# A Mamba block with a mixture of experts on one core: one buffer of delta*u, a last input in four pieces, and the slots of the chunks dealt anew

## What is computed

```python
u, res = split(x @ W_in)                     # 512 channels each
u = silu(three-tap causal convolution of u)
dt, Bm, Cm = split(u @ W_x)                  # 16 + 16 + 16
delta = softplus(dt @ W_dt + b_dt)
for each of 16 states n, along the tokens:
    h_n = exp(delta * A_n) * h_n + (delta * u) * Bm_n
    y  += h_n * Cm_n
y = (y + u * D) * silu(res)
x = layernorm(x + y @ W_out)
```

## Time and profile before

| what | value |
| --- | --- |
| median of 3 runs | 2394.84 us (2394.42 to 2395.79) |
| the profiled execution | 2394.69 us, its span 2392.8 us |
| chunks 0 to 15, first scan to last | 25.2 to 1562 us |
| granted clock of TensorE | 0.977 of full speed, mean over the span |
| busy over the span | PE 94%, PEld 76%, DVE 90%, ACT 73%, POOL 77% |

### The profile page before, as it was taken

One profiled execution on the slowest core, in us unless ns is written; L12 is line 12 of the kernel. 1 busy time (PEld: TensorE's weight loads), 2 busy tenths in 40 slices (PEclk: granted clock), 3 DMA queues, 4 the chain that ended last, 5 costly groups with the idle time before them and its releaser, 6 DMA issues. The chain is left out here.

```text
span 2392.8 us, 39513 instructions
## 1 busy us (share of the span) xinstructions
PE 2245.3 (94%) x14183; PEld 1809.9 (76%) x14183; DVE 2145.2 (90%) x2917; ACT 1746.1 (73%) x2935; POOL 1851.2 (77%) x1028
## 2 busy tenths in 40 slices
PE   9999999999999999999999997745999999999995
PEld 5677777777777777777777766634999999999995
DVE  6999999999999999999999999986787787787775
ACT  6989989999899999998998998842344344434355
POOL 5899999999999999999999999952336437436465
PEclk9999999999999999999999999966999999999998
DMA  3222222222122222221222211122122322322353
GB/s 114 63 62 72 72 80 71 72 71 81 62 72 72 80 71 72 71 81 62 72 72 80 72 63 62 62 71 75 32 67 45 87 65 45 88 64 44 89 200 135
DMA packets 88722, 178.93 MB, mean 75 GB/s; under 512 B 9152, under 2 KB 51904, under 8 KB 88528
## 3 DMA queue, kind: packets, MB, share of 16 engines
q1 hardware_dynamic: 73648, 154.11, 19.4%
q0 software_dynamic: 14880, 22.29, 5.2%
HBM read 140.20 MB, written 36.18 MB: 74 GB/s over the span
## 5 line engine op out<-in xcount | busy, mean ns | idle before, releaser
L1105 DVE TENSOR_TENSOR_SCAN hst<-da,dbu 128x512 f32<-128x512 f32 x1008 | 1173.4, 1209 | 15.5 <-ACT da L806 10.1
L612 POOL TENSOR_TENSOR dbu<-du,b_all 128x2048 f32<-128x2048 f32 x254 | 1154.5, 4546 | 22.3 <-DVE hst L1105 22.3
L806 ACT ACTIVATE da<-delta,a_neg 128x512 f32<-128x512 f32 x1008 | 695.3, 699 | 101.4 <-DVE hst L1105 96.1
L2447 PE MATMUL gu<-x_part,w_part 128*128 128x384 f32 (+1 forms) x2304 | 485.8, 360 | 3.1 <-DVE x_part L2194 1.7
L2447 PEld LDWEIGHTS gu<-x_part,w_part 128*128 128x128 f32 x2304 | 402.9, 189 | 34.1 <-issue 4.5
L1272 PEld LDWEIGHTS hd<-ident,hst 128*128 128x128 f32 x2040 | 240.3, 141 | 187.3 <-issue 121.2
L772 ACT ACTIVATE hTC<-w,c_tok 128x512 f32<-128x512 f32 x510 | 350.1, 687 | 18.1 <-PE w L1272 12.8
L1190 PE MATMUL gen<-xT,w_u 128*128 128x512 f32 x720 | 360.9, 597 | 0.1
L1272 PEld LDWEIGHTS w<-ident,hst 128*128 128x128 f32 x2040 | 243.2, 141 | 142.9 <-issue 97.3
L1272 PE MATMUL hd<-ident,hst 128*128 128x128 f32 x2040 | 312.9, 276 | 35.9 <-DVE yacc L991 27.3
L991 DVE SCALAR_TENSOR_TENSOR yacc<-hd,c_tok,yacc 128x512 f32<-128x512 f32 x457 | 335.0, 733 | 12.6 <-PE hd L1272 7.6
(11 more groups left out here) (348 smaller groups left out, 2829.3 us busy)
## 6 DMA issues: line engine op xcount, KB each, us to landing
b_all<-b_rows SPq DMA_DIRECT2D x128, 512.0 KB, 3.7
xT<-in_xT SPq DMA_DIRECT2D x16, 514.0 KB, 5.0
xT_r<-in_xT SPq DMA_DIRECT2D x16, 512.0 KB, 5.0
x_rows<-in_x SPq DMA_DIRECT2D x16, 512.0 KB, 3.8
w_raw<-in_wg SPq DMA_DIRECT2D x8, 1024.0 KB, 5.0
w_raw<-in_wu SPq DMA_DIRECT2D x8, 1024.0 KB, 8.3
w_raw<-in_wd SPq DMA_DIRECT2D x8, 1024.0 KB, 10.7
x_dram<-x SPq DMA_DIRECT2D x15, 512.0 KB, 3.0
```

Of the source, the lines that this page charges most:

```text
L612: nc.gpsimd.tensor_tensor(dbu[DBU[n]][:], du[parity][:], b_n, ALU.mult).then_inc(dbu_ready, 1)
L806: nc.scalar.activation(da_bank[t % 2][:], delta[parity][:, t, :], ACT.Exp, scale=a_neg[:, t, n:n + 1]).then_inc(da_ready, 1)
L1105: nc.vector.tensor_tensor_scan(hst[DBU[n]][:, t, :], decay[:], dbu[DBU[n]][:, t, :], 0.0, ALU.mult, ALU.add).then_inc(scanned, 1)
L2447: last = nc.tensor.matmul(gu_bank[n % 2][i][:, 0:width(n)], gu_part[wp][:, i, kk, f * P:(f + 1) * P], x_part[xp][:, kk, tokens_of(j)], sta ...
```

## The change

`du` is one buffer. It is written at the very end of a chunk, after state 15's input, and no longer ahead of it. State 15's input is made in four instructions of 512 elements a partition, each waiting for one scan of state 13 and no longer for all four. The place of the second buffer, `held`, takes the scaled block of state 6 instead of `gap`; in chunk 14 the block of state 14 too is scaled and kept (in a free part of the weights `w_u`), where before VectorE added it. The lent-out places move to `dbu[2]`, `w_r` and `xT_r`, with one more wait, in chunk 15. Nearly every slot in the tables is dealt anew.

```diff
 FILL_AT = {
-    "r0": (0, 0, 0), "r1": (1, 0, 6), "C0": (0, 2), "r2": (0, 4, 5), "C1": (0, 6, 8, 9, 10, 12),
-    "r3": (1, 8, 10), "o0": (0, 15, 15, 16, 18), "o1": (1, 21, 22, 23, 23), "xd": (0, 21, 23, 24, 24),
-    "cT": (0, 27), "u0": (1, 24, 29, 30, 32, 33, 34), "d0": (0, 28), "d1": (0, 32), "d2": (0, 35),
-    "u1": (1, 36, 39, 39, 40, 41, 43), "d3": (0, 38), "u2": (1, 45, 47, 47, 47, 48, 49), "ud0": (0, 45),
-    "xt0": (0, 48), "xt1": (0, 53), "u3": (1, 54, 55, 56, 57, 60, 61), "ud1": (0, 54), "lg": (0, 56, 57, 60, 62),
+    "r0": (0, 0, 0), "r1": (1, 0, 5), "C0": (0, 2), "r2": (0, 4, 4), "C1": (0, 7, 8, 10, 10, 13),
+    "r3": (1, 12, 12), "o0": (0, 15, 16, 18, 19), "o1": (1, 21, 22, 23, 23), "xd": (0, 21, 23, 24, 24),
+    "cT": (0, 27), "u0": (1, 24, 29, 30, 31, 33, 35), "d0": (0, 27), "d1": (0, 32), "d2": (0, 35),
+    "u1": (1, 36, 39, 39, 41, 41, 43), "d3": (0, 38), "u2": (1, 45, 45, 47, 47, 48, 50), "ud0": (0, 45),
+    "xt0": (0, 49), "xt1": (0, 52), "u3": (1, 54, 55, 57, 57, 58, 61), "ud1": (0, 54), "lg": (0, 58, 59, 60, 61),
 }
 READ_AT = {
-    "r0": 2, "r1": 8, "C0": 3, "C1": 12, "r2": 6, "r3": 12, "xd": 26, "cT": 28, "u0": 37, "d0": 32, "d1": 35,
-    "d2": 38, "d3": 41, "u1": 46, "ud0": 46, "u2": 53, "xt0": 52, "xt1": 54, "ud1": 55, "u3": 63, "lg": 63,
+    "r0": 2, "r1": 9, "C0": 3, "C1": 12, "r2": 6, "r3": 14, "xd": 26, "cT": 28, "u0": 37, "d0": 32, "d1": 35,
+    "d2": 38, "d3": 41, "u1": 45, "ud0": 46, "u2": 53, "xt0": 51, "xt1": 54, "ud1": 57, "u3": 63, "lg": 63,
 }
-SUM_LATE_AT = 25
+SUM_LATE_AT = 24
-ACC_READ_AT = (7, 12)
+ACC_READ_AT = (8, 9)
-EXP_AT = (42, 47)
-LN_AT = (49, 50)
-NORM_AT = (39, 43, 45, 49)
+EXP_AT = (42, 45)
+LN_AT = (48, 50)
+NORM_AT = (40, 43, 44, 49)
-SMALL_AT = 11
+SMALL_AT = 8
-FIRST_DECAY_AT = 55
+FIRST_DECAY_AT = 57
-STASH = {c: {5: "extra", 6: "gap", 14: "row0"} for c in range(TOK // CL)}
-STASH[CHUNKS - 2] = {5: "w0", 6: "w1"}
+STASH = {c: {5: "extra", 6: "v0", 14: "row0"} for c in range(TOK // CL)}
+STASH[CHUNKS - 2] = {5: "w0", 6: "w1", 14: "w2"}
...
 FIRST_FILL_AT = {
-    "v0": (0, 0, 0, 0, 1, 1, 2), "v1": (1, 0, 0, 2, 2, 3, 3), "v2": (0, 2, 2, 3, 3, 3, 3),
...
-    "xd": (0, 19, 20, 22, 24), "u0": (1, 21, 22, 25, 26, 26, 27), "cT": (0, 33), "d0": (1, 30), "d1": (0, 33),
...
+    "v0": (0, 0, 0, 0, 0, 0, 2), "v1": (1, 0, 0, 0, 2, 2, 2), "v2": (0, 2, 2, 3, 3, 3, 3),
...
+    "xd": (0, 20, 21, 21, 26), "u0": (1, 21, 22, 22, 24, 27, 29), "cT": (0, 32), "d0": (0, 30), "d1": (0, 33),
...
-FIRST_LN_AT = (48, 50)
+FIRST_LN_AT = (49, 51)
...
-        du = [sb(f"du{i}", [P, DT, CL]) for i in range(2)]
+        du = sb("du", [P, DT, CL])
+        held = sb("held", [P, DT, CL])
...
-                    if n == DU_AT and s.front:
+                    if n == NST - 1 and s.front:
 
                         pool.wait_ge(delta_ready, c + 1)
...
-                        pool.wait_ge(u_ready, c + 2)
-                        nc.gpsimd.tensor_tensor(du[other][:], delta[other][:], u[:], ALU.mult).then_inc(du_ready, 1)
...
                         done = n - DBU_BACK[n]
+                        b_n = b_all[n // BG % 2][:, n % BG:n % BG + 1, :]
+                        if n == NST - 1:
+                            for t in range(DT):
+                                pool.wait_ge(scanned, c * SLOTS + DT * done + t + 1)
+                                ins = nc.gpsimd.tensor_tensor(dbu[DBU[n]][:, t, :], du[:, t, :], b_n[:, 0, :], ALU.mult)
+                            ins.then_inc(dbu_ready, 1)
+                        elif done >= 0 or s.close:
+
+                            pool.wait_ge(scanned, c * 64 + 4 * done + 4)
                         if done >= 0 or s.close:
 
-                            pool.wait_ge(scanned, c * 64 + 4 * done + 4)
...
+                if s.front:
+
+                    if s.main:
+                        pool.wait_ge(dbu_ready, (c + 1) * NST)
+                    pool.wait_ge(u_ready, c + 2)
+                    nc.gpsimd.tensor_tensor(du[:], delta[other][:], u[:], ALU.mult).then_inc(du_ready, 1)
...
                         if c == CHUNKS - 1 and slot == TOP_MAX_AT[0]:
                             dve.wait_ge(ring_read, s.base_read())
+                            dve.wait_ge(gate_ready, CHUNKS)
```

More of the change, by code:

```diff
@@ L77 @@
 }
-SMALL_AT = 11
+SMALL_AT = 8
 ADD_AT = 15
-DU_AT = 15
 LAST_ORDER = (0, 2, 1, 3)
@@ L91 @@
 CARRY_HELD = NST - 2
-FIRST_DECAY_AT = 55
-STASH = {c: {5: "extra", 6: "gap", 14: "row0"} for c in range(TOK // CL)}
-STASH[CHUNKS - 2] = {5: "w0", 6: "w1"}
+FIRST_DECAY_AT = 57
+STASH = {c: {5: "extra", 6: "v0", 14: "row0"} for c in range(TOK // CL)}
+STASH[CHUNKS - 2] = {5: "w0", 6: "w1", 14: "w2"}
 STASH[CHUNKS - 1] = {5: "u0", 6: "u1", 7: "u2", 8: "u3", 9: "extra", 10: "w0", 11: "w1", 12: "w2", 13: "w3", 14: "w4"}
 STASH_AT = {
-    0: 6, 1: 11, 2: 14, 3: 19, 4: 21, 5: 26, 6: 30, 7: 34, 8: 38, 9: 42, 10: 46, 11: 50, 12: 55, 13: 58, 14: 62,
+    0: 9, 1: 11, 2: 16, 3: 18, 4: 25, 5: 26, 6: 30, 7: 33, 8: 38, 9: 42, 10: 46, 11: 50, 12: 55, 13: 58, 14: 62,
 }
@@ L131 @@
 FIRST_FILL_AT = {
[5 rows of a table removed]
[5 rows of a table added]
 }
 FIRST_READ_AT = {
-    "r0": 10, "r1": 13, "r2": 15, "r3": 18, "xd": 27, "cT": 33, "u0": 30, "d0": 33, "d1": 35, "d2": 37, "u1": 48,
-    "d3": 40, "ud0": 42, "u2": 59, "ud1": 44, "u3": 63, "v0": 1, "v1": 2, "v2": 7, "v3": 13,
+    "r0": 8, "r1": 13, "r2": 15, "r3": 19, "xd": 28, "cT": 34, "u0": 31, "d0": 32, "d1": 35, "d2": 37, "u1": 48,
+    "d3": 40, "ud0": 42, "u2": 61, "ud1": 45, "u3": 63, "v0": 1, "v1": 3, "v2": 4, "v3": 13,
 }
@@ L304, in attention @@
                       for i in range(N_TAPS * KD)})
+        stash.update({f"v{i}": held[:, i, :].rearrange("p (t q) -> p t q", q=P) for i in range(DT)})
         stash.update({f"x{i}": xT[:, i, 0:CL].rearrange("p (t q) -> p t q", q=P) for i in range(KD)})
@@ L389, in attention @@
         tops = {}
-        for buffer, names in ((delta[0], TOP_WIDE[:4]), (du[0], TOP_WIDE[4:])):
+        for buffer, names in ((delta[0], TOP_WIDE[:4]), (w_r, TOP_WIDE[4:6]), (xT_r, TOP_WIDE[6:])):
             flat = buffer[:].rearrange("p t c -> p (t c)")
@@ L393, in attention @@
                 tops[name] = flat[:, m * EARLY * NE:(m + 1) * EARLY * NE].rearrange("p (t e) -> p t e", e=NE)
-        thin = du[0][:].rearrange("p t (c o) -> p (t c) o", o=1)
+        thin = xT_r[:].rearrange("p t (c o) -> p (t c) o", o=1)
         for m, name in enumerate(TOP_THIN):
-            tops[name] = thin[:, 3 * EARLY * NE + m * EARLY:3 * EARLY * NE + (m + 1) * EARLY, :]
+            tops[name] = thin[:, EARLY * NE + m * EARLY:EARLY * NE + (m + 1) * EARLY, :]
         last_bank = {0: da_bank[0], 2: da_bank[1], 1: hd_bank, 3: gen_bank[0]}
@@ L412, in attention @@
         b_rows = dram["b_rows"]
-        w_staging = du[1][:].rearrange("p a b -> p (a b)")[:, 0:KD * DI].rearrange("p (k d) -> p k d", k=KD)
+        w_staging = dbu[2][:].rearrange("p a b -> p (a b)")[:, 0:KD * DI].rearrange("p (k d) -> p k d", k=KD)
         HALF_PADDED = (SEQ + 2) // 2
@@ L606, in chunk @@
                             for t in range(DT):
-                                ins = nc.gpsimd.tensor_tensor(dbu[DBU[1]][:, t, :], du[0][:, t, :], b_all[0][:, 1, :],
+                                ins = nc.gpsimd.tensor_tensor(dbu[DBU[1]][:, t, :], du[:, t, :], b_all[0][:, 1, :],
                                                               ALU.mult)
@@ L610, in chunk @@
                             continue
-                        b_n = b_all[n // BG % 2][:, n % BG:n % BG + 1, :].to_broadcast([P, DT, CL])
-                        nc.gpsimd.tensor_tensor(dbu[DBU[n]][:], du[parity][:], b_n, ALU.mult).then_inc(dbu_ready, 1)
+                        if n < NST - 1:
+                            nc.gpsimd.tensor_tensor(dbu[DBU[n]][:], du[:], b_n.to_broadcast([P, DT, CL]), ALU.mult
+                                                    ).then_inc(dbu_ready, 1)
                         if parity == 1:
@@ L782, in stash_state @@
                     act.wait_ge(u_ready, CHUNKS)
-                elif s.c == CHUNKS - 1:
+                elif s.c == CHUNKS - 1 or buffer[0] == "v" and s.close:
                     act.wait_ge(ring_full, s.nth_full("C1") + 1)
@@ L964, in lead_terms @@
                 dve.wait_ge(lead_delta, t + 1)
-                nc.vector.tensor_tensor(du[0][:, t, :], delta[0][:, t, :], u[:, t, :], ALU.mult
+                nc.vector.tensor_tensor(du[:, t, :], delta[0][:, t, :], u[:, t, :], ALU.mult
                                         ).then_inc(lead_du if not last else du_ready, 1)
@@ L969, in lead_terms @@
                 dve.wait_ge(lead_du if not last else du_ready, t + 1 if not last else 1)
-                nc.vector.tensor_tensor(dbu[DBU[0]][:, t, :], du[0][:, t, :], b_all[0][:, 0, :], ALU.mult
+                nc.vector.tensor_tensor(dbu[DBU[0]][:, t, :], du[:, t, :], b_all[0][:, 0, :], ALU.mult
                                         ).then_inc(lead_dbu if not last else dbu_ready, 1)
```

## The result

The changed kernel takes 2401.68 us (median of 9 runs, 2401.38 to 2402.70), the kernel before, run beside it, 2394.16 us (9 runs, 2393.67 to 2395.79). The ratio is 1.0032, with an interval of 1.0023 to 1.0041. The forecast was 2400.7 in a range of 2386 to 2405, and "slower" had the largest chance.

The account below looks back on a forecast made before the run. VectorE was taken as the full engine (busy 1326.2 of 1344 us), with GpSimd's chain setting the chunk's end; +8.0 in chunks 1 to 13 and -2.0 in chunk 0 gave +6.0 on 2394.69, so 2400.7, range 2386 to 2405.

Parts of the forecast that it names:

- The decay of slot 46: On ScalarE, the exp and u1's read move ahead of this decay, so scan 46 begins 0.73 us late.
- GpSimd's chain: Inputs up to state 0's at the chunk's end: four pieces and later du add 0.41 us even, 0.55 odd.
- Slot 11: A sum on VectorE, late behind its TensorE turn, comes on time as r3 moves: 0.25 us less a chunk.
- Slot 40: TensorE's turn keeps all that stood before it, so the sum's wait of 0.24 us stays.
- Per chunk: Terms summed over chunks 2 to 12 and 1 to 13: even +0.89 us, odd +0.39, together +8.0.
- Chunk 14: One sum less, worth 0.64 us, sits behind GpSimd's chain: between -0.9 and +0.2, taken as 0.
- Chunk 15: Its new wait, on a gate made 12 slots before, is already met: 0.
- Chunk 0: Moved TensorE parts gain 1.6 us at slot 20, up to 1.0 at slot 30; net -2.0.
- A: Rival: scan 46 isn't late, as ScalarE reaches slot 44 earlier; -3.4 us, 2391.3; chance 0.20.
- B: Rival: scan 46 on time and slot 40's turn also on time; -8.5 us, 2386.2; chance 0.15.
- C: Rival: ScalarE has no slack, slot 46's decay pays the whole 1.43 us; 2409.8; chance 0.11.
- D: Rival: nothing shows, the chain as long as before since du may overlap differently; 2394.8 us; chance 0.04.

Follow-up runs that it names:

- e2: The kernel before with only ScalarE's slots of the change (exp at 45, logarithms, norm blocks, u1's read); ratio to the kernel before 1.0046.
- e8: e2 with the change's places for u2's parts and xt0 as well; ratio to the kernel before 1.0043.
- e9: The changed kernel with u2's parts and xt0 at their old places; ratio to the kernel before 1.0037.
- e4: The kernel before with all the change's slots, du still ahead of state 15's input, that input in one instruction; ratio to the kernel before 1.0012.
- e7: e4 with the exp and the logarithms back at slots 47, 49 and 50; ratio to the kernel before 0.9974.
- e3: The changed kernel with state 15's input in one instruction again; ratio to the kernel before 1.019.
- e1: The changed kernel with the exp and the logarithms back at slots 47, 49 and 50; ratio to the kernel before 1.000.
- e5: The changed kernel with state 0's input also made and waited for in four pieces; ratio to the kernel before 1.0046.

## Why the prediction was right, and where it was not

**The decay of slot 46** (the term that decides): predicted 0.73, measured 0.68 to 0.70 in chunks 1 to 13. It is won back by slot 51 (-0.11, -0.41, -0.19, -0.21), as foretold, and goes on through GpSimd. What the prediction missed is that this winning back is not given: it hangs on u2's parts, which the change happened to move, and which had been costed at nothing "within a full TensorE". Without that move an odd chunk loses 0.25 more (e2 96.35, e8 96.10) or 0.30 more (e9 96.02, the changed kernel 95.72).

**GpSimd's chain**: predicted +0.41 in an even chunk and +0.55 in an odd one. Measured 24.70 - 24.29 = 0.41, and from the sum of delta to the scan after it 419.99 - 400.90 = 19.09 against 414.31 + 4.54 + 0.09 - 400.38 = 18.56 before, 0.53. Four pieces take 4.93 to the start of the next instruction (308.96 to 313.89), one instruction 4.50: each further piece of 512 costs 0.14, as 4.91 in the earlier trace rows had said. The Trainium skill (GPSIMD Engine Reference, section 3.1) gives about 156 ns for the dispatch of one instruction on VectorE and no figure for GpSimd's; the 60 ns a piece that the prediction worked out from the page's other figures are less than half of the 0.14 that the trace shows.

**Slot 11**: predicted -0.25, measured -0.25. **Slot 40**: predicted to stay late, and it does: the sum begins 2.46 after the pair of scans in both kernels. Of the late decay behind it 0.06 came off.

**Per chunk**: even 96.70 to 96.73 against 96.7 or 96.8 by the sum (95.86 + 0.89), odd 95.72 (the median) against 95.79. Six even chunks make +5.1 (predicted 5.3), seven odd ones +2.5 (2.7).

**Chunk 14**: predicted 0, measured +0.29. The sum that was taken away gives 0.64 at slot 61 (as in e4 and e7). State 15's earlier input gives 0.61 at slot 59: before, scan 60 began at 1465.84, 0.09 after that input. But the step into state 0 is 1.75 longer, so both are hidden behind GpSimd, as said. The measured value lies 0.1 above the bounds given (-0.9 to +0.2). "No late decay there" was wrong: scan 46 is 0.24 late, as it is in e2 and e8.

**Chunk 15**: predicted 0, measured +0.5, of it 0.34 at slot 20. There a decay stands behind the making of the gate on ScalarE (L868), which waits for GpSimd's product with the gate before it (L551). The product ended 28.52 after the chunk's first scan before (1500.14) and ends 28.82 after it now (1507.31). GpSimd works without a gap up to it; at the end of chunk 14 it had 0.30 in hand over VectorE before, and has none now. So 0.30 of the 0.34 comes from the longer chain too.

**Chunk 0**: predicted -2.0, measured -1.55, and 0.49 more ahead of its first scan. The slots come out close: slot 20 -1.50 for -1.6, slot 30 -1.11 for -1.0, the longer chain +1.0 for +0.7 (2.07 at the chunk's end less 1.05 at slot 59). A gain of 1.05 at slot 13 was not foreseen, and the 0.5 lost at slots 1 to 7 is the loss that the prediction had put at 0.6 and held to be covered. The 0.49 is no effect of the change: with the same tables e9's first scan begins at 25.13, e3's at 25.84. And the *cause* given for slot 20 was wrong. The 1.6 was put down to TensorE standing at xd's first part with the turn behind it. Here is the stretch from 66 to 68 us in the kernel before, in e2 and in e8, whose tables for chunk 0 are the same (columns as in the earlier trace rows):

```profile
66.00:68.00 2.00, 2.00 (x4) 0.86 (x5) 0.71 (x1) 1.98 (x2) 2.00 (x1) 0.52 0.00 0
```

```profile
66.00:68.00 2.00, 2.00 (x8) 1.02 (x8) 1.16 (x2) 1.98 (x2) 2.00 (x1) 1.00 0.00 0
```

```profile
66.00:68.00 2.00, 1.95 (x4) 0.85 (x5) 0.78 (x1) 1.98 (x2) 2.00 (x1) 0.55 0.00 0
```

The granted clock was 0.52 in one, 1.00 in the next and 0.55 in the third, after the same wait of 1.02 us for u. With the full clock (e2) chunk 0 lasts 106.36 instead of 107.75, without any change to its tables; with the new tables it is 106.20 with the clock full. So of the 1.55 about 1.4 goes with the clock in the traced execution of the kernel before. Whether the new order itself keeps the clock up is not shown: in all eight traces with the new tables it stayed at 1.00 there, with the old ones in one of three. The matmul in the earlier trace rows, 1.96 for two where 1.02 is usual, said so already; the prediction read it as a wait.

**The sum** was +6.0, and the span grew by 6.8: +5.1 + 2.5 + 0.3 + 0.5 - 1.55 + 0.5 (ahead of the first scan) is 7.4 to the last scan, and the rest is 0.6 shorter. The medians differ by 7.5. Part of the nearness is luck: the new tables of chunk 0 are worth about 0.2 at a full clock (106.36 to 106.20), and the clock made it 1.55. Without that 1.4, and without the 0.5 ahead of the first scan, my estimate of the growth of the span is 6.8 + 1.4 - 0.5 = 7.7, still within the range.

**The rivals.** A and B fall: scan 46 is late in every chunk from 1 to 13. C falls: the slack in the earlier trace rows was there. D falls: the chain grew by its 0.41. The claim under the forecast, that state 0's scan follows GpSimd's last link by 0.09 in both kinds of chunk, holds at every chunk's end. That the time follows from it is shown by e1 in both kinds (there too it is 0.09 throughout) and by e5 and e7 in the even ones.

What stays open: chunk 11 took 0.25 more than the other odd ones, in e1 as well. In both, GpSimd begins du 0.36 after the start of the small instruction ahead of it (1180.41 to 1180.77) and not 0.16 as in the other chunks (987.95 to 988.11 in chunk 9), and this chain sets the chunk's end. Why du starts later there is not shown.

## What to carry to other kernels

When one engine's order is moved to an earlier slot, price what the moved instruction delays on its own engine, then follow the delayed product to the engine whose chain closes the loop: 0.7 us that VectorE won back within five slots was paid in full through a scan that releases GpSimd. Look also at what is queued behind each instruction that will now wait, for two matmuls behind a late turn decided whether the delay could be won back. And before a stall is explained by the order of work, read the granted clock of its stretch.
